# First layers' foldings cut up in the first step, and a new passage from the last step to the experts

## The reference

```
def block(h, p):                              # 4 layers, weights of their own
    k, q, v = split(h @ Wkqv, 3)
    r = tril(q @ k.T / sqrt(256)) / row_norm
    r = r / clip(abs(r.sum(-1)), 1.0)
    a, gate = split((r @ v) @ Wm1 + bm1, 2)
    m = groupnorm(a * silu(gate) @ Wm2 + bm2)  # moments over (S, D) of a sequence
    y = m + h
    return layernorm(gelu(y @ Wf1 + bf1) @ Wf2 + bf2 + y)
x = layernorm(x + layers(x))
gates = entmax_1.5(x @ Wr + br)               # 8 experts, over each token
out = sum_e gates[:, e] * (relu(x @ W1[e] + b1[e]) @ W2[e] + b2[e])   # 256 -> 1024 -> 256
x = layernorm(x + out)
```

## Time and profile before

| | |
|---|---|
| runs of the kernel | 2512.55 us, median of 3 (2511.71 to 2513.12) |
| profiled execution | 2511.62 us, of it a span of 2509.9 from the first to the last instruction |
| mean granted TensorE clock | 0.989 |
| busy, share of the span | PE 97%, PEld 81%, DVE 63%, ACT 55%, POOL 54% |

### The profile page before, as it was taken

The page is one execution under the profiler, slowest core; times in us unless marked ns, Lnnn a source line. Parts: engine busy times, 40 slices in busy tenths (PEclk is TensorE's granted clock), DMA queues, the critical chain, the costliest instruction groups (busy, mean ns, idle before and its releaser), DMA issues. The chain is left out here.

```text
span 2509.9 us, 35414 instructions
## 1 busy us (share of the span) xinstructions
PE 2435.6 (97%) x11766; PEld 2031.9 (81%) x11766; DVE 1570.7 (63%) x2880; ACT 1370.8 (55%) x2412; POOL 1359.9 (54%) x1256
## 2 busy tenths in 40 slices
PE   7999999999999999988999999999999999999997
PEld 5788888887888888876888878888888888888886
DVE  1566666666666666777777874675646656565545
ACT  4566666666666666654555544444444444444443
POOL 2255564445444654465788865555645556554554
PEclk9999999999999999988999999999999999999999
DMA  5111101000211112014666554543445444444441
GB/s 163 65 34 33 34 29 65 29 25 30 75 33 33 34 43 68 26 66 142 215 222 203 180 208 171 181 155 139 164 164 178 158 156 146 157 156 163 147 155 72
DMA packets 104582, 283.45 MB, mean 113 GB/s; under 512 B 7024, under 2 KB 77056, under 8 KB 88064
## 3 DMA queue, kind: packets, MB, share of 16 engines
q1 hardware_dynamic: 104320, 281.75, 32.5%
q10 hardware_dynamic: 128, 0.03, 0.0%
HBM read 212.16 MB, written 69.60 MB: 112 GB/s over the span
## 5 line engine op out<-in xcount | busy, mean ns | idle before, releaser
L653 POOL TENSOR_TENSOR hid_lo<-full,hid_hi 128x512 fp32r<-128x512 f32 x384 | 500.9, 1319 | 537.7 <-ACT full L926 471.3
L1380 DVE SCALAR_TENSOR_TENSOR full<-ps,bias_cols,sum 128x512 f32<-128x512 f32 x384 | 288.3, 751 | 223.1 <-PE ps L1626 203.1
L1624 PE MATMUL ps<-hid_hi,m_w 128*128 128x512 f32 x1024 | 402.2, 393 | 0.2 <-ACT z L860 0.2
L1626 PE MATMUL ps<-hid_hi,m_w 128*128 128x512 f32 x1024 | 399.1, 390 | 0.0
L1625 PE MATMUL ps<-hid_lo,m_w 128*128 128x512 f32 x1024 | 398.8, 389 | 0.0
L923 ACT ACTIVATE hid_hi<-ps,bias_cols 128x512 fp32r<-128x512 f32 x128 | 88.3, 690 | 502.0 <-PE ps L1626 502.0
L1624 PE MATMUL ps<-te_hi,m_w 128*128 128x512 f32 x896 | 352.0, 393 | 5.4 <-DVE sum L1367 3.9
L1626 PE MATMUL ps<-te_hi,m_w 128*128 128x512 f32 x896 | 349.2, 390 | 0.0
L1625 PE MATMUL ps<-te_lo,m_w 128*128 128x512 f32 x896 | 349.1, 390 | 0.0
L585 POOL TENSOR_TENSOR pf_sp<-tmp,pf_sp 128x512 fp32r<-128x512 f32 x128 | 163.7, 1311 | 143.2 <-ACT pf_sp L847 143.2
L930 ACT ACTIVATE hid_hi<-full 128x512 fp32r<-128x512 f32 x256 | 161.7, 632 | 121.7 <-DVE full L1380 121.7
(11 more groups left out here) (203 smaller groups left out, 5681.6 us busy)
## 6 DMA issues: line engine op xcount, KB each, us to landing
m_w<-prepared SPq DMA_DIRECT2D x96, 1408.0 KB, 6.0
prepared<-m_w SPq DMA_DIRECT2D x32, 1408.0 KB, 5.8
h_store<-h_out SPq DMA_DIRECT2D x32, 512.0 KB, 3.2
we_raw<-in_L_ffn_W SPq DMA_DIRECT2D x64, 256.0 KB, 6.4
gate_bc<-gate_rows SPq DMA_DIRECT2D x64, 256.0 KB, 6.3
h_in<-h_store SPq DMA_DIRECT2D x24, 512.0 KB, 4.5
h_in<-in_L_attn_x SPq DMA_DIRECT2D x8, 512.0 KB, 5.1
raw<-in_L_attn_Wf SPq DMA_DIRECT2D x8, 512.0 KB, 7.6
```

The costliest lines, as they stand in the source:

```text
L653: nc.gpsimd.tensor_tensor(out=hid_lo[:, k, :], in0=full[:, k, :], in1=f32(hid_hi[:, k, :]), op=ALU.subtract).then_inc(hid_ready, 1)
L1380: nc.vector.scalar_tensor_tensor(out=full[:, k, :], in0=src, scalar=b1_col(e, 2 * fp + BLOCK_ROW[k]), in1=other[:, :], op0=ALU.add, op1=AL ...
L1624: nc.tensor.matmul(out, w[0], x[0], start=first, stop=False, skip_group_check=True)
L1626: return nc.tensor.matmul(out, w[1], x[0], start=False, stop=last, skip_group_check=True)
```

## The change

It edits two places, and the buffers that they need.

- First step. The operands of each fold get buffers outside of `y`, `z` and `h_out` (folds 0 and 3 share one set, folds 1 and 2 have one each), k and q of layer 0 are loaded first, then x, and folds 1 and 2 are loaded without waiting for the fold before. The folds are cut into transposes, first product and second product, and these are written between the parts of slot A's first step.
- Last step and passage. One half of `normalise_x1`, `low_weights(0)`, `sum_weights(0)` and `(1)` and one `inverse_root` move up into the last body. Behind it, the two column blocks of slot B's gated projection are issued apart, with transposes between; the routing quarters stand two ahead of and two behind `group_moments`, products 0 to 2 behind them, products 3 to 6 behind the up projection; out and down projection run with the operand's block as the outer loop. GpSimd waits for `y_ready` between token halves 2 and 3. VectorE has `low_weights(1)`, then `second_sum`, `compare_scores` and `third_sum`. `transpose_gates` moves to the end of quad 1, and the layer norms of three tensors move to quads 1 to 9.

```
 sync, program start:
-            load_fold_operands(0)
+            load_part(0, 0, kq_loaded)
+            load_part(0, 1, kq_loaded)
+            sp.dma_start(floor[:, :], score_floor).then_inc(consts_loaded, DMA)
             load_x(A_, 0)
+            load_part(0, 2, vm_loaded)
+            load_m1(0, vm_loaded)
+            load_fold_operands(1)
             load_plain_weights(0)
-            sp.dma_start(floor[:, :], score_floor).then_inc(consts_loaded, DMA)
+            load_fold_operands(2)
             load_x(B_, 0)
...
 sync, passage:
-            sp.wait_ge(r_psum[B_], DONE)
+            sp.wait_ge(m2_psum[A_], DONE)
             load_weights(0)
+            sp.wait_ge(y_ready[A_], DONE)
             load_weights(1)
...
 gpsimd, body:
+                if last:
+                    sum_weights(0)
                 mask_scores(B_, now, range(TB))
                 split_f(A_, now)
+                if last:
+                    sum_weights(1)
...
 gpsimd, passage:
-            sum_weights(0)
-            layernorm_out(pool, nc.gpsimd, B_, STEP_BEFORE)
-            for m in range(5):
+            for m in range(3):
                 low_token(0, m)
             rstd_group(B_, LAST_STEP)
-            for m in (5, 6):
+            pool.wait_ge(y_ready[B_], DONE)
+            for m in range(3, 7):
                 low_token(0, m)
-            sum_weights(1)
-            layernorm_rstd(A_, LAST_STEP)
-            sum_weights(2)
             split_f(B_, LAST_STEP)
...
 vector, body:
                 low_r(A_, now)
                 if last:
                     sum_moments(0, 1)
+                    normalise_x1(0, 0)
...
                 if last:
-                    for t in range(2):
-                        normalise_x1(0, t)
+                    normalise_x1(0, 1)
                 for half in range(2):
                     divide(B_, now, half)
+                if last:
+                    low_weights(0)
                 low_r(B_, now)
...
 vector, passage:
             groupnorm_in(B_, LAST_STEP)
             groupnorm_var(B_, LAST_STEP)
+            groupnorm_out(B_, LAST_STEP)
+            low_weights(1)
             second_sum(0)
-            groupnorm_out(B_, LAST_STEP)
-            for blocks in HALVES:
-                layernorm_stats(A_, LAST_STEP, blocks)
-            layernorm_var(A_, LAST_STEP)
-            third_sum(0)
-            block_sum(0, C22)
-            low_weights(1)
-            normalise_last(A_, LAST_STEP)
-            layernorm_out(dve, nc.vector, A_, LAST_STEP)
             for part in range(2):
                 compare_scores(0, part)
-            block_sum(0, C21)
-            block_sum(0, C12)
+            third_sum(0)
+            for k in (C22, C21, C12):
+                block_sum(0, k)
...
 vector, quads (the halves of the same layer norm behind each other):
+                if w == 2:
+                    layernorm_gain(dve, nc.vector, B_, STEP_BEFORE, z[B_][:, :, :])
+                if w == 8:
+                    layernorm_gain(dve, nc.vector, A_, LAST_STEP, z[A_][:, :, :])
+                if w == 9:
+                    layernorm_gain(dve, nc.vector, B_, LAST_STEP, z_end)
...
 tensor, body of the first step:
                 transpose_h(A_, now)
+                if not before:
+                    fold_qk(0)
+                    transpose_v(0)
+                    pe.wait_ge(consts_loaded, 7 * DMA)
...
+                    fold_vm(0)
                 for c in range(DC):
                     project_t(A_, now, c)
...
-                    fold(1)
+                    transpose_kq(1)
                 scores(A_, now, (0, 1))
                 scores(A_, now, (2, 3))
+                if not before:
+                    transpose_v(1)
+                    fold_qk(1)
+                    fold_vm(1)
                 retain(A_, now)
...
-                    fold(2)
+                    transpose_kq(2)
+                    transpose_v(2)
+                    fold_qk(2)
                 transpose_r(A_, now)
...
+                    fold_vm(2)
                 gated_projection(A_, now)
...
 tensor, passage:
+            gated_projection(B_, LAST_STEP, (0,))
             for j in (2, 3):
                 transpose_x1(0, j)
-            gated_projection(B_, LAST_STEP)
+            gated_projection(B_, LAST_STEP, (1,))
             transpose_z(A_, LAST_STEP)
...
-            for quarter in range(4):
+            out_projection_end()
+            for quarter in range(2):
                 route(0, quarter)
-            out_projection(B_, LAST_STEP)
+            group_moments(B_, LAST_STEP)
+            for quarter in range(2, 4):
+                route(0, quarter)
             for n in range(3):
                 product(0, n)
-            group_moments(B_, LAST_STEP)
-            for n in (3, 4):
+            up_projection(B_, LAST_STEP)
+            for n in range(3, 7):
                 product(0, n)
-            up_projection(B_, LAST_STEP)
-            for n in (5, 6):
-                product(0, n)
-            for c in range(DC):
-                down_projection(B_, LAST_STEP, c)
-            transpose_z(B_, LAST_STEP)
+            down_projection_end()
```

More of the change, by code:

```diff
@@ L221, in we_lo, with fold_operands @@
             return slots[q % RING][:, 1, :]
-        raw_kqv = [y[B_][:, 0, :], y[B_][:, 1, :], z[B_][:, 0:DC, :].rearrange("p c d -> p (c d)")]
-        raw_m1 = h_out[B_][:, :, :].rearrange("p k d -> p (k d)").rearrange("p (c n) -> p c n", c=DC)
+        def fold_operands(l):
+            if l % 3 == 0:
+                whole = [place(f"fold_kqv{l}_{i}", [P, D * DC], LAST[B_] + i * 2 * KB) for i in range(3)]
+                return whole, place(f"fold_m1_{l}", [P, DC, MC * P], LAST[B_] + 8 * KB)
+            at = WORK[B_] + 256 + (36 if l == 1 else 20) * KB
+            return ([place(f"fold_kqv{l}_{i}", [P, D * DC], at + i * 2 * KB) for i in range(3)],
+                    place(f"fold_m1_{l}", [P, DC, MC * P], at + 6 * KB))
+        raw_kqv, raw_m1 = zip(*(fold_operands(l) for l in range(L)))
         w_t = tmp[B_][:, 0:3, :]
+        staging = [raw, raw, place("fold_staging", [P, FOLD], WORK[B_] + 36 * KB + 256), raw]
         ps = ctx.enter_context(nc.psum_tensor("ps", [P, 8, 512], F32))
@@ L673, in body @@
                     split_weight("vm", now.layer)
-                if not before:
-                    split_weight("m2", 0)
                 mask_scores(A_, now, (0,))
@@ L1008, in body @@
                 high_f(A_, now, FC - 1)
+                if last:
+                    high_weights(0)
                 keep_r(B_, now, range(TB))
@@ L1601, in _ @@
                     block_sum(w + 1, C12)
+                if w == 0:
+                    for part in (1, 2):
+                        find_support(0, part)
+                if w == 2:
+                    layernorm_bias(dve, nc.vector, B_, STEP_BEFORE, z[B_][:, :, :])
+                if w in (4, 5):
+                    layernorm_var(w - 4, LAST_STEP)
+                if w == 8:
+                    layernorm_bias(dve, nc.vector, A_, LAST_STEP, z[A_][:, :, :])
+                if w == 9:
+                    layernorm_bias(dve, nc.vector, B_, LAST_STEP, z_end)
                 finish_last(p - 1, i, LATE)
@@ L1724, in out_projection, with out_projection_end, down_projection_end @@
                     ins.then_inc(m2_psum[s], 2)
+            def out_projection_end():
+                w = weight("m2", DC)
+                for k in range(DC):
+                    pe.wait_ge(u_lo[B_], LAST_STEP.base + 2 * k + 2)
+                    for c in range(DC):
+                        ins = mm3(bank(B_, OUT[c]), both(w, ALL, k, cols(c)), both(tu_sp[B_], ALL, k), k == 0, k == DC - 1)
+                        if k == DC - 1:
+                            ins.then_inc(m2_psum[B_], 2)
+            def down_projection_end():
+                w = weight("f2", FC)
+                pe.wait_ge(f_ready[B_], LAST_STEP.base + DC)
+                for k in range(FC):
+                    pe.wait_ge(f_lo[B_], LAST_STEP.base + k + 1)
+                    for c in range(DC):
+                        ins = mm3(bank(B_, c), both(w, ALL, k, cols(c)), both(pf_sp[B_], ALL, k), k == 0, k == FC - 1)
+                        if k == FC - 1:
+                            ins.then_inc(f2_psum[B_], 2)
             def group_moments(s, at):
@@ L1894, in body @@
                     up_projection(B_, before, (1,))
+                else:
+                    fold_vm(2)
                 gated_projection(A_, now)
@@ L1922, in first @@
             def first(now):
-                fold(0)
-                pe.wait_ge(consts_loaded, 7 * DMA)
-                nc.tensor.transpose(bank(A_, 0)[:, 0:L * LC], const_rows[:, :], ident[0:L * LC, 0:L * LC]).then_inc(const_psum, 1)
+                transpose_kq(0)
                 body(now, None, False)
@@ L1957, in _ @@
                         product(w + 1, n)
+                    if w == 0 and n == 0:
```

(1 more changed line is left out.)

314 lines of the change are left out of this document (184 added, 130 removed).

## The result

The changed kernel takes 2473.66 us, the median of 4 runs (2471.77 to 2476.91), beside 2512.84 for the kernel before (4 runs, 2511.71 to 2513.27): ratio 0.9849, interval 0.9837 to 0.9860. That is 39.2 us less; the prediction said 2479.5, with 2472 to 2491 for the range.

What follows compares the result with a forecast made beforehand. TensorE, busy 97% of the span, was taken as the bound, leaving only waits and low clock. Start 11.7 plus passage 21.9 made 33.6 off 2511.62: 2478.0, median 2478.9, stated as 2479.5; range 2472 to 2491.

Steps and rivals of the forecast that it cites:

- The start: First step up to slot B's transposes: cut folds fed earlier bring them from 72.2 to 60.5, gain 11.7 us.
- Early loads cost nothing: First step: loading folds 1 and 2 early, 2.5 MB ahead of what stood there, costs nothing.
- the rival of crowded transfers: First step: 6.1 MB asked for at once delays x to 14; start gives 5.7 or less, 2487 to 2490; chance 0.09.
- Both took 5.61 us; with 2.8 ...: Last body, VectorE: one m_xs normalisation moves away, the other takes 2.8 us, so TensorE does not wait for y.
- the rule's other half: VectorE instructions with two SBUF inputs contend with GpSimd reading SBUF; compare_scores' second part stays at 1.65 us each.
- The 4.00 us wait: Passage: TensorE's wait for ry_sp shrinks to 0.2 us, since GpSimd's wait for y_ready leaves VectorE the port.
- the walk: Passage, along TensorE's queue from 1092.3: out projection done at 107.2, routing and products at 113.1 (1000 left off).
- the prediction's own price: Passage, VectorE's chain for y: a 128x2 operation takes 1.25 us beside GpSimd's halves, 0.22 in the step before.
- the 3 us put down for the low clock after routing: Passage: TensorE's clock falls again after the routing products, costing 3 us, bounds 0 and 3.4.
- The new wait: After the up projection: TensorE waits 0.5 and 4.0 us for third_sum behind VectorE's queue, then 2.5 us at low clock.
- just in time: First quads: gates come as their later-placed transpose needs them, 0.4 us loss allowed, 9.0 us gained.
- 16.9 less 3: Passage up to slot B's first product: 16.9 us gained, less 3 us for the low clock after routing.

Runs made afterwards that it cites:

- 14.0 alone: Kernel before with only the first step's part of the change (loads, buffers, cut folds): 2497.15 us beside 2511.16, 14.0 less.
- experiment 3: Changed kernel with operands of folds 1, 2 and 3 loaded only once the fold before is out of TensorE: 2494.92 us, ratio 0.9929.
- Experiment 5: Changed kernel with third_sum, alone or with one or all three block sums, ahead of compare_scores' second part on VectorE: 2474.00, 2472.93, 2473.34 us.
- third_first: Changed kernel with third_sum between the two parts of compare_scores on VectorE: 2474.00 us, ratio 0.9853.
- after_again: The changed kernel run once more, unaltered, beside the other variants: 2473.10 us.
- compare_late: Changed kernel with third_sum and all three block sums of the first quad ahead of compare_scores' second part: 2473.34 us, ratio 0.9848.

## Why the prediction was right, and where it was off

**The bound.** Right: all of the gain lies in the first 58 us, in the passage, and in the first quads; the layers took 1014.6 for 1013.6.

**The start, 11.7 forecast, 14.5 in the trace, 14.0 alone.** k and q came at 4.69 (4.5 forecast), x at 7.5 (8.0; the lower bound of 7.0 does not follow from its own terms, q's landing at 4.5 and 0.5 MB at 3.7 us per MB, which give 6.4), the transposes for slot B at 57.74 (60.5). The working was 0.5 us late at x and 1.5 at the second product (14.15 for 15.7), the latter as the clock rose inside the first product (3.03 us, not 3.8); another 1.3 lies in the rest. "Early loads cost nothing" held, and experiment 3 shows what the sentence left out: without them nothing of the start's gain is left. Of the rival of crowded transfers nothing came.

**The wait for `y`: forecast gone, measured 1.27 us.** The step that failed is "Both took 5.61 us; with 2.8 ...", half of a group whose members did not cost the same. Of the eight operations the three beside GpSimd's `split_f` took 1.37 to 1.40 us and the others 0.40. The three slow ones stood in the half that the change moved away; the half that stayed, 0.40 each before, came up into their place beside `split_f` (1072.73 to 1077.89) and became slow: 4.74 us, so 0.9 saved, not 2.8. The price went with the place, not with the instruction. The Trainium skill, "SBUF — State Buffer", Who interferes with whom, names this case: a `tensor_scalar` that runs in a 2-port mode contends with GpSimd even with one SBUF input. The rows agree as to the contention (0.40 us without, 1.38 beside it), but that these operations ran in such a mode no row shows. The prediction had weighed only the rule's other half.

**`ry_sp`.** The 4.00 us wait went, as forecast, and the three small operations fell to 0.2 each as forecast. But the way from the out projection to the up projection is 8.5 us (1095.76 to 1104.27), not the 5.9 of the walk: 107.2 to 113.1. It is the chain over VectorE, GpSimd and ScalarE that sets it, not TensorE's work: the products of `group_moments` began 2.8 us behind the out projection (1.8 forecast), and `y` and `ry_sp` took 5.7 from there (4.2). Of the first, 0.8 is the prediction's own price at a place it did not look at: the 128x2 operation on `gin` took 0.97 us beside GpSimd's token halves, 0.16 in the kernel before. With that the 3 us put down for the low clock after routing should not have been added: the clock did fall there (0.50 to 0.72 granted from 1100 to 1104), but VectorE had written the first low half of `ry_sp` only at 1104.20, and the up projection began at 1104.27. At a full clock TensorE would have waited for it instead.

**The new wait.** Named at its place, with 4.5 us in two pieces; it was 3.09; 0.6 of the difference is `compare_scores`, 4.1 us (1109.95 to 1114.05) and not 4.7. The clock fell behind it as forecast (0.51 granted from 1114.0 to 1120.5). Experiment 5 shows that removing it brings no gain that the medians can tell, and that behind it stand `full` and then the gates.

**`pf_sp`, gates, layer norms.** `split_f` was done at 1117.66, the down projection began at 1117.55, and nothing waits for it. The gates are ready at 1146.60 and transposed at 1146.65: "just in time" was exact, with 9.4 us gained in the experts for the 9.0 less 1 forecast. The 1 us for three layer norms was nothing: from 1150 to 2455 TensorE waits for 2.5 us in all; in the kernel before, from 1180 to 2490, for 2.6.

Trace against trace the sum is 14.5 - 1.0 + 11.8 + 9.4 = 34.7, beside 33.6 forecast; the terms that missed (start +2.8, passage to slot B's transposes -2.1 against 16.9 less 3, gates and layer norms +1.4, layers -1.0) nearly cancel. In part that is luck: without the 3 us for the clock the walk up to slot B's transposes had 16.9 and the trace 11.8, and that term, which cost nothing in its place, stood in for 3 of the 5.1 us that `y` (1.3), the way to the up projection (2.6) and, on balance, smaller steps cost.

**What the sum left out, 4.5 us of the median.** Of the 5.8 us between 2479.5 and the median of 2473.66, 1.1 is the sum, 1.5 what was added for the median and the refill, and 3.3 the distance of the changed kernel's profiled execution from its median. Other runs of the changed kernel had spans down to 2470.0 at a mean granted clock of 0.995, the profiled one 2475.2 at 0.993. Profiles that came out low show where such time lies. The layers are the same in the changed kernel and in `third_first` (span 2469.6), and TensorE waits for 1.9 to 2.1 us at the same four places in both: at 288 us for GpSimd's weight halves and at about 335, 600 and 867 us for `ry_sp`. Windows of 10 us around or right behind these waits, of the changed kernel and then of `third_first`:

```profile
285.00:295.00 10.00, 7.97 (x33) 6.23 (x32) 6.22 (x6) 5.43 (x9) 5.71 (x4) 0.83 0.41 141
...
330.00:340.00 10.00, 7.99 (x43) 6.47 (x42) 8.61 (x15) 4.64 (x11) 2.91 (x2) 1.00 0.00 0
...
600.00:610.00 10.00, 8.28 (x34) 6.88 (x35) 6.99 (x19) 6.99 (x15) 3.01 (x9) 0.83 0.00 0
865.00:875.00 10.00, 8.12 (x35) 6.71 (x34) 8.54 (x23) 5.42 (x12) 2.50 (x9) 0.83 0.01 2
```

```profile
285.00:295.00 10.00, 8.57 (x43) 7.30 (x44) 6.59 (x12) 5.78 (x9) 5.85 (x3) 1.00 0.32 106
330.00:340.00 10.00, 7.92 (x36) 6.63 (x35) 8.61 (x23) 5.35 (x12) 2.56 (x9) 0.83 0.00 0
600.00:610.00 10.00, 10.00 (x58) 8.75 (x59) 7.34 (x23) 8.29 (x19) 6.01 (x12) 1.00 0.00 0
860.00:870.00 10.00, 8.15 (x36) 6.87 (x36) 8.84 (x15) 4.63 (x10) 3.53 (x7) 0.83 0.01 2
```

The changed kernel fell after three of the waits, `third_first` after two (335 and 865). The layers of `third_first` took 1012.8 in place of 1014.6, and its first fold's product 1.89 us in place of 3.03, with slot B's transposes at 56.17. `after_again` fell after three as well, in a layers' time of 1014.4, and `compare_late` after all four, in 1015.9: a fall is worth about 1.6 us here, not the 3.3 expected, and the count explains only a part of the spread. Of the spans of one program, 2470.0 to 2475.2, the rest lies at least in part in the start. That the whole gains 38 to 39 where its parts gain 34.1 may be this; in the traces the parts have more than the whole (36.2 and 34.7), so no coupling of the two is shown, and it was not settled.

## What to carry to other kernels

Before half of a group of instructions is priced at half its time, look at its members one by one, and at what another engine does beside them: an operation that moves into the place of a slow one can become as slow. When work is cut up so that it can start earlier, its operands are wanted earlier too, and the prefetch is the gain: here 14.5 us with it and a loss of 3.7 without. Where three engines' queues meet within 5 us, moving one item trades one wait for the next (`sum3`, `full`, gates, in turn); when what is left is less than one program varies by from run to run (here 5 us), a trace can show the wait gone and the time cannot confirm it.

## What the runs showed of the hardware

- A VectorE operation beside a GpSimd one on SBUF: `tensor_scalar` of 128x256 took 1.38 us in place of 0.40, one of 128x2 1.22 in place of 0.23. The low weights (128x1408, two inputs) took 2.71 beside GpSimd and 1.61 mostly without it; four statistics of 128x256 took 1.40 and 1.39 us in the two places tried, both beside GpSimd.
- The same wait of TensorE was followed by the lower clock in one execution and not in the next: after 2.03 us at 288 us it fell in the changed kernel (0.83) and not in `third_first` (1.00), at about 335 the other way round. Removing the 1.27 us wait for `y` left the stretch as long as it was, at a granted clock of 0.87 for 0.90. In the kernel before, the clock fell behind the waits that the prediction lists, but the matmuls behind the 1.85 us wait follow each other at 0.23 us, as at the upper level.
- 0.75 MB more asked for ahead of x on the same queue made it 3.0 us later.
- In the first 10 us the granted clock is shown as 1.00, while eight transposes take 1.94 us, as at the lower level, and 1.09 at the upper: at the start of a program durations tell the level better than that column.
